# Second attention: each values call in two halves, and part of the next stage run inside its last units

## The reference

```python
x = _layernorm(x + _L0_attn_ref(x, ...))   # causal, 16 heads of 128
x = _layernorm(x + _L0_ffn_ref(x, ...))    # 8 experts, top 2, and a shared one
x = _layernorm(x + _L1_attn_ref(x, ...))   # 16 query heads of 16, keys and values in 4 groups
x = _layernorm(x + _L1_ffn_ref(x, ...))    # 16 experts, top 6, and a shared one
```

```python
scores = jnp.einsum('bqhd,bkhd->bhqk', q, k) / HD
prob = jax.nn.softmax(scores, axis=-1)
out = jnp.einsum('bhqk,bkhd->bqhd', prob, v).reshape(b, s, D)
return out @ Wout + bout
```

## Time and profile before

| what | value |
|---|---|
| median of three runs | 2173.84 us (2172.9 to 2176.99) |
| the profiled execution: its time | 2171.24 us |
| its span, first to last instruction | 2169.1 us |
| mean granted TensorE clock, as a share of full speed | 0.986 |
| busy, share of the span | PE 96%, DVE 67%, ACT 56%, POOL 27% |

### The profile page before, as it was taken

One profiled execution on the slowest core, in us unless ns is written; L12 is line 12 of the kernel. 1 busy time (PEld: TensorE's weight loads), 2 busy tenths in 40 slices (PEclk: granted clock), 3 DMA queues, 4 the chain that ended last, 5 costly groups with the idle time before them and its releaser, 6 DMA issues. The chain is left out here.

```text
span 2169.1 us, 31294 instructions
## 1 busy us (share of the span) xinstructions
PE 2093.0 (96%) x11136; PEld 1596.3 (74%) x11136; DVE 1452.7 (67%) x2761; ACT 1211.7 (56%) x2435; POOL 577.9 (27%) x679
## 2 busy tenths in 40 slices
PE   7999999999999999989999989999998899999997
PEld 6888888888888888877788863333333678778886
DVE  5666666667666776666656568888883556655555
ACT  5666666666556666644444444777777434444343
POOL 3444444444334444422222210000000112222221
PEclk9999999999999999999999996999999999999999
DMA  2000000000000000011111120000000111111111
GB/s 74 20 21 20 13 21 20 21 20 20 9 20 21 21 20 21 16 31 39 44 44 44 44 53 14 17 21 18 19 20 2 43 34 47 41 47 37 51 52 56
DMA packets 54301, 64.78 MB, mean 30 GB/s; under 512 B 9179, under 2 KB 34566, under 8 KB 54150
## 3 DMA queue, kind: packets, MB, share of 16 engines
q1 hardware_dynamic: 54150, 62.81, 10.6%
HBM read 52.68 MB, written 2.10 MB: 25 GB/s over the span
## 5 line engine op out<-in xcount | busy, mean ns | idle before, releaser
L861 POOL TENSOR_TENSOR a_pr<-a_pr,a_rinv 128x512 f32<-128x512 f32 (+3 forms) x384 | 312.8, 829 | 477.8 <-DVE a_rinv L1108 477.8
L86 PE MATMUL psum<-xh,g_hi_gu 128*128 128x512 f32 x928 | 377.8, 407 | 15.4 <-DVE xl L1091 9.2
L88 PE MATMUL psum<-xh,g_lo_gu 128*128 128x512 f32 x928 | 363.8, 392 | 0.0
L87 PE MATMUL psum<-xl,g_hi_gu 128*128 128x512 f32 x928 | 363.1, 391 | 0.0
L1782 DVE TENSOR_REDUCE a_negm<-psum 128x1 f32<-128x1024 f32 x256 | 301.5, 1220 | 36.3 <-PE psum L1660 35.5
L1189 POOL TENSOR_TENSOR g_lo_gu<-g_raw_gu,g_hi_gu 128x512 fp32r<-128x512 f32 x84 | 108.9, 1296 | 796.2 <-ACT g_hi_gu L1185 796.2
L1763 ACT ACTIVATE a_pt<-psum 128x512 f32<-128x512 f32 x512 | 268.2, 603 | 81.4 <-PE psum L1675 81.1
L1483 DVE TENSOR_TENSOR f_hl<-f_hid,f_hh 128x512 fp32r<-128x512 f32 x168 | 116.9, 696 | 238.2 <-ACT f_hh L1421 236.3
L1410 ACT ACTIVATE f_act_s<-psum,g_gu_bias 128x512 f32<-128x512 f32 x168 | 115.0, 685 | 276.4 <-PE psum L88 276.1
L1013 ACT ACTIVATE a_pr<-psum,a_negm 128x128 f32<-128x128 f32 (+7 forms) x256 | 190.3, 743 | 106.7 <-DVE a_negm L1098 102.7
L1020 ACT ACTIVATE a_pth<-psum 128x512 fp32r<-128x512 f32 (+3 forms) x384 | 174.8, 490 | 113.2 <-PE psum L920 109.6
(11 more groups left out here) (290 smaller groups left out, 4307.5 us busy)
## 6 DMA issues: line engine op xcount, KB each, us to landing
g_raw_gu<-in_gu SPq DMA_DIRECT2D x84, 256.0 KB, 2.8
f_raw_dn<-in_down SPq DMA_DIRECT2D x84, 128.0 KB, 2.0
g_raw_gu<-in_qkv SPq DMA_DIRECT2D x32, 256.0 KB, 2.8
a_wvr<-in_qkv SPq DMA_DIRECT2D x32, 128.0 KB, 2.4
a_wor<-in_o SPq DMA_DIRECT2D x32, 128.0 KB, 2.1
x_queries_qq<-x_qhi SPq DMA_DIRECT2D x128, 32.0 KB, 2.0
yT<-in_xT SPq DMA_DIRECT2D x4, 512.0 KB, 6.4
x_queries_qq<-x_qlo SPq DMA_DIRECT2D x64, 32.0 KB, 1.9
```

The costliest lines, as they stand in the source:

```text
L86: pe.matmul(out, a_hi, b_hi, start=first, stop=False)
L87: pe.matmul(out, a_hi, b_lo, start=False, stop=False)
L88: return pe.matmul(out, a_lo, b_hi, start=False, stop=last)
L861: pool.tensor_tensor(x, x, rinv[:, j:j + 1].to_broadcast([P, count * P]), ALU.mult).then_inc(p_done, 1)
```

## The change

- Each call of `values` is cut in two: columns 0 to 255 of the four outputs in an even step, 256 to 511 in the odd step after it. Each half now stands at the beginning of its step, before the maxima and scores. The waits of a call are now in its first half.
- Four `zt` and four `op` tasks of the output projection of batch 0, and the four `FORE` tasks of its norm, leave the lead of the last mixture and stand in the last 24 steps of the attention, at steps REAR0 + 1, 2, 4, ... (REAR0 is step 8 of unit 14), on each engine behind the step's own work. Their ring is the double bank of `mx_ps` that no maximum needs any more; the turns keep to the other one (`Slots`, `left_over`). Their rounded z goes into the tiles of batch 0's queries, which are no longer needed.
- The lead keeps `root`, `BACK` and the two logits; `split` is 1 (`root`).
- A norm's place in the semaphore counts comes from a list of names; the norm's tiles move to an outer phase.

```diff
--- before.py
+++ after.py
@@ -99,7 +99,6 @@
         self.uses, self.roundings = 0, 0
         self.mv_done, self.std_done = sem("norm_mv_done"), sem("norm_std_done")
         self.rstd_done, self.xn_done = sem("norm_rstd_done"), sem("norm_xn_done")
-        self.norms = 0
         self.shifted, self.exp_done = sem("router_shifted"), sem("router_exp_done")
         self.step, self.weights_done = sem("router_step"), sem("router_weights_done")
         self.routers, self.exps, self.steps = 0, 0, 0
@@ -150,6 +149,9 @@
     if ring.room(key) > 0:
         pe.wait_ge(ring.emptied, ring.room(key))
     return ring.bank(key)
+
+
+NORMS = ["n0a", "n0b", "n1a", "n1b", "n2a", "n2b", "n3a", "n3b"]
 class NormHalf:
@@ -168,8 +170,7 @@
         self.ready = lambda s, ring: ()
         self.mv_done, self.std_done = counters.mv_done, counters.std_done
         self.rstd_done, self.xn_done = counters.rstd_done, counters.xn_done
-        self.nth = counters.norms
-        counters.norms += 1
+        self.nth = NORMS.index(name)
     @staticmethod
     def has_bank(t):
@@ -1537,7 +1538,7 @@
             self.fetch(sp, u)
-def grouped_attention(nc, tag, queries, sides, ks, vs, z, ident, psum):
+def grouped_attention(nc, tag, counters, queries, sides, ks, vs, z, ident, psum, rear):
@@ -1600,23 +1601,50 @@
             def __init__(self):
-                self.n, self.maxima, self.turns = 0, 0, 0
-                self.freed = []
+                self.n, self.maxima = 0, 0
+                self.freed = [None, None]
             def place(self):
-                self.n += 1
-                return (self.n - 1) % 2, self.freed[self.n - 3] if self.n > 2 else None
+                if self.maxima < len(UNITS) * STEPS:
+                    self.n += 1
+                    return (self.n - 1) % 2, self.freed[(self.n - 1) % 2]
+                return self.n % 2, self.freed[self.n % 2]
             def a_max(self):
                 at = self.place()
                 self.maxima += 1
-                self.freed.append(((mx_taken, self.maxima),))
+                self.freed[at[0]] = ((mx_taken, self.maxima),)
                 return at
             def a_turn(self, u, with_z, with_m):
                 at = self.place()
-                self.freed.append((((z_done, u),) if with_z else ()) + (((m_kept, u + 2),) if with_m else ()))
+                self.freed[at[0]] = (((z_done, u),) if with_z else ()) + (((m_kept, u + 2),) if with_m else ())
                 return at
+
+        def left_over():
+
+            slots = Slots()
+            for u, i in FIRST:
+                slots.a_max()
+                if (u, i) == (0, STEPS - 1):
+                    slots.a_turn(-1, False, True)
+            for u in range(LAST + 1):
+                for i in range(STEPS):
+                    if maxima_at(u, i):
+                        slots.a_max()
+                        if slots.maxima == len(UNITS) * STEPS:
+                            return 1 - slots.n % 2, slots.freed[1 - slots.n % 2]
+                    if i == TURN and (u > 0 or u < LAST):
+                        slots.a_turn(u, u > 0, u < LAST)
+
+        SPARE, SPARE_FREE = left_over()
+        rear_ring = Ring(counters, [mx_ps[:, SPARE, k, :] for k in range(2)])
+        enlist(rear_ring, [t for n, t in rear])
+        REAR0 = (LAST - 1) * STEPS + STEPS // 2
+
+        def rear_at(u, i):
+
+            return [t for n, t in rear if REAR0 + n == u * STEPS + i]
         @block.sync
         def _(sp):
@@ -1675,17 +1703,20 @@
                 pe.matmul(st_ps[:, n % 3, :], ks[b][p0:p0 + ROWS + 1, g % 2, kt * P:(kt + 1) * P],
                           qq[p0:p0 + ROWS + 1, u % QSLOT, g % 2, :], start=True, stop=True).then_inc(st_ready, 1)
-            def values(n):
+            def values(n, half):
                 u, kt = n // NK, n % NK
                 b, j, c = UNITS[u]
-                pe.wait_ge(exp_done, (n + 1) * G1)
-                if kt == 0 and u >= 1:
+                x = slice(half * CH // 2, (half + 1) * CH // 2)
+                if half == 0:
+                    pe.wait_ge(exp_done, (n + 1) * G1)
+                if kt == 0 and half == 0 and u >= 1:
                     pe.wait_ge(zt_done, u)
                 for g in range(G1):
-                    m = pe.matmul(acc_ps[g * W:(g + 1) * W, :], vs[b][:, kt, g, :], pt[:, n % SLOTS, g, :],
-                                  start=kt == 0, stop=kt == NK - 1, tile_position=(0, g * W))
-                m.then_inc(pv_done, 1)
+                    m = pe.matmul(acc_ps[g * W:(g + 1) * W, x], vs[b][:, kt, g, :], pt[:, n % SLOTS, g, x],
+                                  start=kt + half == 0, stop=kt + half == NK, tile_position=(0, g * W))
+                if half == 1:
+                    m.then_inc(pv_done, 1)
             def turn(u, with_z, with_m, bank):
                 if with_z:
@@ -1705,19 +1736,25 @@
                     turn(-1, False, True, room(ring.a_turn(-1, False, True)))
             for u in range(LAST + 1):
                 for i in range(STEPS):
+                    if u * NK + i // 2 >= LAG:
+                        values(u * NK + i // 2 - LAG, i % 2)
                     ahead = maxima_at(u, i)
                     if ahead:
                         bank = room(ring.a_max())
                     for k in range(2):
                         if ahead:
                             maxima(*ahead, k, bank)
-                        if k == 1 and i % 2 == 1 and u * NK + i // 2 >= LAG:
-                            values(u * NK + i // 2 - LAG)
                         scores(u, i, k)
                     if i == TURN and (u > 0 or u < LAST):
                         turn(u, u > 0, u < LAST, room(ring.a_turn(u, u > 0, u < LAST)))
+                    for side, t in rear_at(u, i):
+                        if (side, t) == rear[0][1]:
+                            for sem, n in SPARE_FREE:
+                                pe.wait_ge(sem, n)
+                        side.tensor(pe, t, rear_ring)
             for n in range(LAG):
-                values((LAST + 1) * NK - LAG + n)
+                for half in range(2):
+                    values((LAST + 1) * NK - LAG + n, half)
             turn(LAST + 1, True, False, room(ring.a_turn(LAST + 1, True, False)))
         @block.scalar
@@ -1766,6 +1803,8 @@
                         keep_z(u - 1)
                     if i == TURN and u < LAST:
                         keep_maxima(u + 1)
+                    for side, t in rear_at(u, i):
+                        side.scalar(act, t, rear_ring)
             keep_z(LAST)
         @block.vector
@@ -1808,6 +1847,8 @@
                         bank = ring.a_turn(u, u > 0, u < LAST)[0]
                         if u > 0:
                             keep_z(u - 1, bank)
+                    for side, t in rear_at(u, i):
+                        side.vector(dve, t, rear_ring)
             keep_z(LAST, ring.a_turn(LAST + 1, True, False)[0])
@@ -1924,9 +1965,14 @@
             gu1 = GateUp(g, "gu1", w1, raw_gu, hi_gu, lo_gu)
             causal_attention(nc, "a0", counters, a, xh, xl, yT, ident, idr, eps, psum, rw0, n0a, r0a, gu0)
+            def follows(n, o):
+
+                n.ready = lambda s, ring: ((ring.emptied, ring.count((o.name, ("op", s // 2, DT - 1)))),)
+
             z = [g.sb(f"z{b}", [P, S // P, D]) for b in range(B)]
             wo = Projection(g, "wo", a["wo1"], a["bo1"])
             rw1 = RouterWeights(g, "rw1", w1, False)
+            n2a = norm(g, "n2a", 0)
             with Phase(nc, "x") as x:
                 wqkv = Projection(x, "wqkv", a["wqkv1"], a["bqkv1"])
                 x.level(0)
@@ -1956,25 +2002,21 @@
                     kv, khi, klo = (o[:].rearrange("p s n -> p (s n)") for o in (raw_gu, hi_gu, lo_gu))
                     x1 = QKVHalf(s, "x1", 1, wqkv, kv, khi, klo, xh, xl, ident, "n1b").into(qhi[1], qlo[1], ks[1], vs[1])
                     in_turn(nc, "p1", counters, psum, tasks(n1b, FORE + [("root",)] + BACK) + tasks(x1, PROJECT), (x1, wo, rw1, queries))
-                    grouped_attention(nc, "a1", queries, (x0, x1), ks, vs, z, ident, psum)
-
-            def follows(n, o):
-
-                n.ready = lambda s, ring: ((ring.emptied, ring.count((o.name, ("op", s // 2, DT - 1)))),)
+                    o1a = OutHalf("o1a", 0, wo, z[0], qhi[0], qlo[0], xh, xl, yT, ident, idr)
+                    follows(n2a, o1a)
+                    order = [TURN[0], TURN[1], GATHER[0], GATHER[1], TURN[2], TURN[3], GATHER[2], GATHER[3]]
+                    rear = list(zip((1, 2, 4, 6, 8, 9, 11, 13, 15, 17, 19, 21), tasks(o1a, order) + tasks(n2a, FORE)))
+                    grouped_attention(nc, "a1", counters, queries, (x0, x1), ks, vs, z, ident, psum, rear)
             with Phase(nc, "s2") as s:
                 zh = s.sb("zh", [P, DT, S], F32R)
                 zl = s.sb("zl", [P, DT, S], F32R)
-                def out_half(name, b):
-                    return OutHalf(name, b, wo, z[b], zh, zl, xh, xl, yT, ident, idr)
-
```

(11 more changed lines are left out.)

## The result

The changed kernel takes **2246.09 us** (2245.33 to 2247.27, four runs), the kernel before 2173.37 beside it: ratio 1.0336, interval 1.0321 to 1.035, so 3.4% slower. The forecast was 2170.6 with a range to 2184. The profiled execution has a span of 2243.8, against 2169.1.

What follows compares the result with a forecast made beforehand. It took PE and ACT, waiting for each other in turn, to bound the attention, and PE afterwards. Terms -0.5 - 1.0 + 11.7 - 13.4 = -3.2 gave 2168.0 profiled, plus 2.6 for the median: 2170.6 us, range 2155 to 2184.

Steps and rivals of the forecast that it cites:

- a new stall of 1.55 in each unit: Second attention, step 4: first half call waits 1.55 us for ACT's copy of z, taking back the halves' 1.4 a unit.
- Side work, where it goes: Last 24 attention steps: twelve moved tasks cost +11.7 us, bounds -1.2 to +13.3, as PE has no cover.
- the step: Second attention: a PE step with half calls takes 0.56 + 0.33 + 0.33 = 1.22 us, against 1.305 before.
- the lead: Start of the last mixture until its first gate weights: 9.7 us instead of 23.06, so -13.4 us.
- unit 0: First attention unit, no copy to wait for: twelve steps with values save 0.085 each, -1.0 us.
- a step of PE was to bind: Second attention after the change: PE's step of 1.22 us becomes the bound, DVE needing only 1.14.
- Dearer halves: Rival, slower: second set of weights shows in each half call, step 1.27, time 2183 us; chance 0.18.
- DVE binds: Rival, faster: tile-mode switch overlaps more, attention step falls to 1.16, -15, time 2155 us; chance 0.17.
- No stall at step 4: Rival, faster: ACT gets its copy in early, 14 x 1.55 = 21.7 less, time 2149 us; chance 0.05.
- Side work hidden: Rival, faster: PE waits in the last steps cover about 10 of the 11.7 us, time 2161; chance 0.10.

Runs made afterwards that it cites:

- e11: Changed kernel with ACT's copy of z between the two exponentials of step 3 instead of after them; 2172.13 us, ratio 0.9987 to the kernel before.
- e4: Changed kernel with values calls still halved but the side work left in the lead; 2255.7 us, ratio 1.0373 to the kernel before.
- e1: Changed kernel with ACT's copy of z moved ahead of both exponentials of step 3; 2163.41 us, ratio 0.9957 to the kernel before.
- e8: Changed kernel with z copied before step 3's exponentials and unit 0 in whole values calls; 2155.55 us, ratio 0.9898 to the kernel before.
- e10: e8 with whole values calls again in the last 24 steps, where the side work stands; 2152.23 us, ratio 0.991 to the kernel before.
- e7: Changed kernel with whole values calls in their old place and z copied between step 5's exponentials; 2208.73 us, ratio 1.0142 to the kernel before.
- e2: Changed kernel with six repeated maxima before the waiting call, and values calls behind their step's bank wait; 2212.22 us, ratio 1.0187 to the kernel before.
- e5: Changed kernel with z copied before step 3's exponentials and the side work left in the lead; 2163.54 us, ratio 0.9933 to the kernel before.

## Why the prediction was wrong

**The step that failed: "a new stall of 1.55 in each unit", priced as 1.55.** The stall is there, in place and length (1.53, ended by the copy of z). It was booked as idle time alone, and the sum went on at full clock. The first paragraph of the prediction noted that the clock is granted and did not ask whether the change puts that at risk. With a gap of 1.04 (e11) units 1 to 13 cost 281.32; 13 x 0.49 more of idle time makes 287.7, which is what the forecast's way of pricing gives for the changed kernel. The one unit in which the clock held through the full gap (e4, unit 7: 22.13) says the same: 13 x 22.13 = 287.7. The other 357.11 - 287.7 = **69.4 us is half clock**. A second way to it: a mean clock of 0.77 between levels of 0.50 and 1.00 puts 46% of 357.11, 164 us, at half clock, where a step takes 2.17 for 1.23 and so 0.43 of the time is lost: 71.

That the gap sets the loss off is shown: halves without it hold the clock (e1, e8 to e10), whole calls with it lose it in six units (e7), a shorter one keeps it (e11), and e2's matmuls in the gap keep it in units 3 to 13. What it then costs is not the gap's doing alone: 69.4 / 13 = 5.3 us for each fall with half calls, and some 15 / 6 = 2.5 with whole ones (e7, where the gap also stands a step later; the 15 is worked out at the end).

On this the Trainium skill (TensorE: Matmul & The Clock Gate, A second HAM failure mode: psum-queue depth-cycling) tells of a kernel in which frequent short idles of TensorE between groups of matmuls let the clock swing, and the falls and rises of the clock cost throughput. The trace agrees at gaps of 1.53 and 1.55 us; at 1.04 (e11) nothing of the kind was seen.

**Side work, where it goes: +11.7 forecast, +18.3 measured.** e11 has 53.55 there; with 0.49 more of gap that is 54.0, +12.3, and the mechanism's size was right within 0.6. The remaining 6 is unit 14's gap, behind which the clock stands at 0.50 to 1724.

```profile
1708.00:1712.00 4.00, 2.72 (x22) 1.14 (x24) 2.24 (x2) 2.22 (x5) 0.00 (x0) 0.83 0.00 0
1712.00:1716.00 4.00, 4.00 (x26) 1.13 (x24) 2.36 (x2) 2.17 (x4) 0.00 (x0) 0.50 0.00 0
...
1724.00:1730.00 6.00, 6.00 (x39) 3.04 (x34) 1.39 (x2) 3.80 (x8) 0.00 (x0) 0.97 0.01 1
```

**Right:** the step (1.22 forecast, 1.23, which is also what DVE takes, below) and the lead (-13.4, -13.5). With the half clock taken out (69.4 and 6.0) the profiled execution, 2245.86, would have taken 2170.5, where the forecast for it was 2168.0; most of the difference is units 1 to 13, 22.13 each where the forecast had 21.92. **Luck:** unit 0 (-1.0, -1.3), for the same unit-0 code took 24.8 to 32.1 in e1, e4, e5 and e11. **Half right:** a step of PE was to bind and DVE to have slack at 1.14. At full clock DVE's maxima run at 1.23 without a break (three in 3.69, above; the 1.14 was read from pairs) and PE's maxima wait for them (e10), so the two stand level. That a narrower step alone would help is therefore not shown.

**The rivals.** *Dearer halves* had the sign and not the cause: the step did not grow. *DVE binds* fell with its price, a step of 1.16, though DVE does stand level at 1.23. *No stall at step 4* is e1's mechanism; e1 took 2163.41 for its 2149, and units 0 and 1 of its profiled execution alone took 12 more than unit 0 of the changed kernel and a unit of 20.91. *Side work hidden* fell: it costs 8 to 12. None of them named the clock.

## What to carry to other kernels

A wait on TensorE costs its idle time and perhaps the clock after it: when a change makes a stall that recurs, price it once at full clock and once with the steps after it at the half-clock duration that some row of the trace shows, and give the second a chance. When a list of waits fills with engines that wait for PE, look at the granted clock stretch by stretch before explaining any of them. If moving one copy ahead of its step takes the stall away (e1), or half a step shortens it enough (e11), make that move with the change, not after it.

## What the runs showed of the hardware

- A gap of 1.53 to 1.56 us in PE's work lowered the clock in 31 of 39 units (13 of 13 in the changed kernel and 12 of 13 in e4, with half calls; 6 of 13 in e7, with whole ones); gaps of 1.04 (e11) and 0.47 (e2) did so in none of 13 and 11. Length alone does not decide: the 0.96 in unit 0 of e2 did lower it, and an idle of 1.59 or 1.60 in the last mixture left it at 1.00 in all twelve profiles. In the kernel before (the idle, and what follows):

```profile
1736.60:1738.20 1.60, 0.02 (x1) 0.00 (x0) 1.60 (x3) 0.61 (x1) 0.41 (x1) 1.00 0.00 0
1738.20:1744.00 5.80, 5.79 (x30) 4.87 (x31) 3.20 (x5) 1.50 (x4) 0.74 (x1) 1.00 0.12 27
```

- Why the same gap tells in one unit and not in another (two neighbouring units of e7) no run settles, nor why the clock stays down longer with half calls: 69 us lost in thirteen units of the changed kernel, and 319.62 - 285.54 - 13 x 1.44 = 15 in e7.
- The attention begins at half clock in every run, and stays there though PE works without a break (10.00 of 10.00 us in e1's first row). Where in unit 0 it rises differs between runs of one unit-0 code: unit 0 took 22.0, 24.8, 31.8 and twice 32.1 with half calls, and 23.3, 23.3, 24.9, 25.5, 25.5 and 28.1 with whole ones. That is up to 10 us from run to run and may be what spreads e11's runs; its cause is open.
